# Retained values with tokens on the partitions: row sums as a column, division in ScalarE's copy, TensorE transposes back

## The reference, cut to what matters

```python
def _retention(x, wkqv):
    k, q, v = jnp.split(x @ wkqv, 3, axis=-1)
    qkt = jnp.einsum('bid,bjd->bij', q, k) / jnp.sqrt(jnp.float32(d))
    row_norm = 1.0 + jnp.sqrt(jnp.arange(s, dtype=x.dtype))[None, :, None]
    r = jnp.tril(qkt) / row_norm
    denom = jnp.clip(jnp.abs(r.sum(-1, keepdims=True)), 1.0, None)
    r = r / denom
    return jnp.einsum('bij,bjd->bid', r, v)

def block(h, p):
    r = _retention(h, wk)
    m = r @ w1 + b1
    a, gate = jnp.split(m, 2, axis=-1)
    m = a * jax.nn.silu(gate) @ w2 + b2
    m = _groupnorm1(m, gg, gb)
    y = m + h
    f = jax.nn.gelu(y @ wf1 + bf1_, approximate=False) @ wf2 + bf2_
    return (_layernorm(f + y, lg, lb), None)
```

## Time and profile before

| | before |
|---|---|
| median of three runs | 2643.9 us |
| profiled execution, time / span | 2644.7 / 2642.9 us |
| mean granted clock of TensorE | 0.978 |
| TensorE matmul / weight load busy | 94% / 78% |
| VectorE / ScalarE / GpSimd busy | 66% / 50% / 52% |
| retention layers | from 0 to about 1210 us |
| a regular body | 68.9 us |

### The profile page before, as it was taken

One profiled execution on the slowest core, in us unless ns is written; L12 is line 12 of the kernel. 1 busy time (PEld: TensorE's weight loads), 2 busy tenths in 40 slices (PEclk: granted clock), 3 DMA queues, 4 the chain that ended last, 5 costly groups with the idle time before them and its releaser, 6 DMA issues. The chain is left out here.

```text
span 2642.9 us, 35142 instructions
## 1 busy us (share of the span) xinstructions
PE 2493.1 (94%) x11574; PEld 2052.7 (78%) x11574; DVE 1739.8 (66%) x2906; ACT 1333.7 (50%) x2288; POOL 1362.8 (52%) x1258
## 2 busy tenths in 40 slices
PE   7999999999999999984899999999999999999997
PEld 5788778887888778862677778878888788888886
DVE  2677777778777877764667774656646556455445
ACT  3465655565555655543455554444444444444443
POOL 2244554444444554445577785455654546554544
PEclk9999999999999999996999999999999999999999
DMA  5100001001200010004565554443344434344441
GB/s 160 61 32 32 32 24 63 19 31 32 72 32 32 32 40 32 24 16 140 187 211 181 171 202 179 168 156 143 146 179 159 165 122 166 140 169 164 144 165 68
DMA packets 99962, 283.54 MB, mean 107 GB/s; under 512 B 6384, under 2 KB 76416, under 8 KB 83456
## 3 DMA queue, kind: packets, MB, share of 16 engines
q1 hardware_dynamic: 99712, 282.01, 30.7%
q10 hardware_dynamic: 128, 0.03, 0.0%
HBM read 212.42 MB, written 69.60 MB: 107 GB/s over the span
## 5 line engine op out<-in xcount | busy, mean ns | idle before, releaser
L1333 POOL TENSOR_TENSOR hid_lo<-full,hid_hi 128x512 fp32r<-128x512 f32 x384 | 498.4, 1311 | 569.4 <-ACT full L1436 459.4
L1614 DVE SCALAR_TENSOR_TENSOR full<-m_ps,bias_cols,sum 128x512 f32<-128x512 f32 x384 | 288.2, 750 | 215.5 <-PE m_ps L1715 201.5
L1713 PE MATMUL m_ps<-hid_hi,m_w 128*128 128x512 f32 x1024 | 403.5, 394 | 0.2 <-POOL hid_lo L1333 0.2
L1715 PE MATMUL m_ps<-hid_hi,m_w 128*128 128x512 f32 x1024 | 401.4, 392 | 0.0
L1714 PE MATMUL m_ps<-hid_lo,m_w 128*128 128x512 f32 x1024 | 401.3, 392 | 0.0
L1713 PE MATMUL m_ps<-m_t_hi,m_w 128*128 128x512 f32 x896 | 355.5, 397 | 27.8 <-DVE full L1614 17.5
L1714 PE MATMUL m_ps<-m_t_lo,m_w 128*128 128x512 f32 x896 | 351.6, 392 | 0.0
L1715 PE MATMUL m_ps<-m_t_hi,m_w 128*128 128x512 f32 x896 | 351.6, 392 | 0.0
L1433 ACT ACTIVATE hid_hi<-m_ps,bias_cols 128x512 fp32r<-128x512 f32 x128 | 88.3, 690 | 495.3 <-PE m_ps L1715 495.3
L322 POOL TENSOR_TENSOR pf_lo<-tmp,pf_hi 128x512 fp32r<-128x512 f32 x128 | 161.6, 1296 | 168.0 <-ACT pf_hi L498 168.0
L1440 ACT ACTIVATE hid_hi<-full 128x512 fp32r<-128x512 f32 x256 | 161.9, 632 | 164.0 <-DVE full L1614 163.8
(11 more groups left out here) (195 smaller groups left out, 5664.1 us busy)
## 6 DMA issues: line engine op xcount, KB each, us to landing
m_w<-prepared SPq DMA_DIRECT2D x96, 1408.0 KB, 6.0
prepared<-m_w SPq DMA_DIRECT2D x32, 1408.0 KB, 5.8
h_store<-h_out SPq DMA_DIRECT2D x32, 512.0 KB, 3.2
m_raw<-in_L_ffn_W SPq DMA_DIRECT2D x64, 256.0 KB, 6.4
gate_bc<-gate_rows SPq DMA_DIRECT2D x32, 512.0 KB, 6.7
h_in<-h_store SPq DMA_DIRECT2D x24, 512.0 KB, 4.3
h_in<-in_L_attn_x SPq DMA_DIRECT2D x8, 512.0 KB, 5.1
raw<-in_L_attn_Wf SPq DMA_DIRECT2D x8, 512.0 KB, 8.1
```

Source lines behind the costliest of these rows:

```text
L1333: nc.gpsimd.tensor_tensor(out=hid_lo[:, k, :], in0=full[:, k, :], in1=f32(hid_hi[:, k, :]), op=ALU.subtract).then_inc(hid_ready, 1)
L1614: nc.vector.scalar_tensor_tensor(out=full[:, k, :], in0=src, scalar=b1_col(e, 2 * fp + BLOCK_ROW[k]), in1=other[:, :], op0=ALU.add, op1=AL ...
L1713: nc.tensor.matmul(out, w[0], x[0], start=first, stop=False, skip_group_check=True)
L1715: return nc.tensor.matmul(out, w[1], x[0], start=False, stop=last, skip_group_check=True)
```

## The change

Retained values are now computed with tokens on the partitions. For each query block k, the stationary operand is the masked score block and the moving one is h, widened by a column of ones (and one for evenness), so that column 256 of the result is the row sum. VectorE makes divisor and reciprocal for 128 x 1 (or 128 x 2) values. ScalarE copies each block out of PSUM and scales it by the reciprocal of its token (`keep_r`). TensorE transposes the copies back (`transpose_r`), eight 128 x 128 blocks per slot. The products of `gated_projection` come out already divided, so `scaled` is gone, and silu and the gated product read PSUM. `up_projection` of slot B and the two calls of `down_projection` of slot A are parted, with `transpose_r` between their halves.

```diff
-        h_sp = split_tiles("h", [P, TB, D])
+        h_sp = split_tiles("h", [P, TB, D + 2])
+            def keep_r(s, at, blocks):
+                for k in blocks:
+                    act.wait_ge(scale_done[s], at.it * SCALE_CHAIN + (3 if k < 2 else 3 * k))
+                    nc.scalar.activation(r_tok[s][:, k, :], score_bank(s, k)[:, 0:D], ACT.Copy, scale=den[s][:, 1, k:k + 1]).then_inc(r_kept[s], 1)
             def high_r(s, at):
                 for c in range(DC):
-                    act.wait_ge(r_psum[s], at.base + 2 * c + 2)
+                    act.wait_ge(rT_psum[s], at.base + 2 * c + 2)
...
-                act.wait_ge(gate_scaled[s], at.base + 2 * c + 2)
-                nc.scalar.activation(tmp[s][:, 2 + c, :], tmp[s][:, 2 + c, :], ACT.Silu,
+                act.wait_ge(m_psum[s], at.base + 2 * c + 1)
+                nc.scalar.activation(tmp[s][:, 2 + c, :], bank(s, GATE[c]), ACT.Silu,
...
                     for c in range(DC):
                         high_y(B_, before, c)
+                    keep_r(A_, now, range(TB))
                     high_r(A_, now)
...
                 high_f(A_, now, FC - 1)
+                keep_r(B_, now, range(TB))
                 load_table(ACT.Silu)
                 high_r(B_, now)
...
-            def divisor(s, at):
...
+            def divide(s, at):
                 base = at.it * SCALE_CHAIN
...
+                for n, (k, width) in enumerate(((0, 2), (2, 1), (3, 1))):
+                    r = (2 + k) % 4
+                    sums = ps[:, 4 * s + r:4 * s + r + width, D]
+                    dve.wait_ge(r_psum[s], at.base + k + width)
+                    landed(nc.vector.tensor_tensor(out=den[s][:, 0, k:k + width], in0=sums, in1=floor[:, k:k + width], op=ALU.max),
+                           scale_done[s], base + 3 * n + 1)
+                    landed(nc.vector.scalar_tensor_tensor(out=den[s][:, 0, k:k + width], in0=sums, scalar=-1.0, in1=den[s][:, 0, k:k + width],
+                                                          op0=ALU.mult, op1=ALU.max), scale_done[s], base + 3 * n + 2)
+                    nc.vector.reciprocal(den[s][:, 1, k:k + width], den[s][:, 0, k:k + width]).then_inc(scale_done[s], 1)
...
             def gated_products(s, at, meanwhile=lambda part: None):
-                scaled(s, at, 0, GATE, 2, 1, gate_scaled)
-                scaled(s, at, 0, VALUE, 0, 2, value_scaled)
+                gated(s, at, 0)
                 meanwhile(0)
-                gated(s, at, 0)
-                scaled(s, at, 1, GATE, 2, 1, gate_scaled)
                 low_u(s, at, 0)
-                scaled(s, at, 1, VALUE, 0, 2, value_scaled)
                 gated(s, at, 1)
...
-                divisor(A_, now)
+                divide(A_, now)
                 low_r(A_, now)
-                invert(A_, now)
...
             def retain(s, at):
...
+                pe.wait_ge(h_lo[s], at.base + U)
+                for k in range(TB):
+                    pe.wait_ge(p_masked[s], at.base + k + 1)
+                    for b in range(k + 1):
+                        ins = mm3(score_bank(s, k)[:, 0:D + 2], both(pf_sp[s], ALL, b, cols(k)), both(h_sp[s], ALL, b), b == 0, b == k)
+                    ins.then_inc(r_psum[s], 1)
+
+            def transpose_r(s, at):
+                for k in range(TB):
+                    pe.wait_ge(r_kept[s], at.base + max(k + 1, DC))
                     for c in range(DC):
...
+                        ins = nc.tensor.transpose(bank(s, 2 + c)[:, cols(k)], r_tok[s][:, k, cols(c)], ident[:, :])
+                        if k == TB - 1:
+                            ins.then_inc(rT_psum[s], 2)
...
                 retain(A_, now)
                 if before:
-                    up_projection(B_, before)
+                    up_projection(B_, before, (0,))
                 else:
                     fold(2)
+                transpose_r(A_, now)
+                if before:
+                    up_projection(B_, before, (1,))
                 gated_projection(A_, now)
...
                 retain(B_, now)
-                for c in range(DC):
-                    down_projection(A_, now, c)
+                down_projection(A_, now, 0)
+                transpose_r(B_, now)
+                down_projection(A_, now, 1)
```

More of the change, by code:

```diff
@@ L124, in retention_layers @@
         z = slot_tiles("z", [P, TB, D])
-        inv = [t[:, 0, :] for t in y]
+        r_tok = [t[:, :, :].rearrange("p c (k d) -> p (c k) d", d=D) for t in y]
+        den = slot_tiles("den", [P, 2, TB])
         warm = sb("warm", [P, 1])
@@ L315, in _ @@
                                     base=0, pattern=[[-1, P]], channel_multiplier=1).then_inc(pool_consts, 1)
-            nc.gpsimd.memset(f32(ones_r[:, :]), 1.0).then_inc(pool_consts, 1)
+            for s in range(SLOTS):
+                nc.gpsimd.memset(f32(h_sp[s][0][:, :, D:D + 2]), 1.0).then_inc(pool_consts, 1)
+                nc.gpsimd.memset(f32(h_sp[s][1][:, :, D:D + 2]), 0.0).then_inc(pool_consts, 1)
             nc.gpsimd.memset(neg_half[:, :], -0.5).then_inc(pool_consts, 1)
             nc.gpsimd.memset(mean_w[:, :], 1.0 / (P * DC)).then_inc(pool_consts, 1)
-            pool.wait_ge(pool_consts, 5)
+            pool.wait_ge(pool_consts, 8)
             def low_half(lo, full, hi, done, n):
@@ L554, in body @@
                 else:
+                    keep_r(A_, now, range(TB))
+                    empty_fold(2)
                     high_r(A_, now)
-                    empty_fold(2)
                 load_table(ACT.Silu)
@@ L675, in gated @@
             def gated(s, at, c):
-                dve.wait_ge(value_scaled[s], at.base + 2 * c + 2)
+                dve.wait_ge(m_psum[s], at.base + 2 * c + 2)
                 dve.wait_ge(gate_ready[s], at.base + 2 * c + 2)
                 nc.vector.scalar_tensor_tensor(
-                    out=tmp[s][:, c, :], in0=tmp[s][:, c, :], scalar=lc_bm1[s][:, c:c + 1],
+                    out=tmp[s][:, c, :], in0=bank(s, VALUE[c]), scalar=lc_bm1[s][:, c:c + 1],
                     in1=tmp[s][:, 2 + c, :], op0=ALU.add, op1=ALU.mult).then_inc(u_ready[s], 2)
@@ L829, in body @@
                     layernorm_var(B_, before)
-                divisor(B_, now)
+                divide(B_, now)
                 low_r(B_, now)
-                invert(B_, now)
             def first(now):
@@ L929, in retain @@
             def retain(s, at):
-                def weighted_h(b):
-                    q = slice(LO[b], S)
-                    for c in range(DC):
[L934 to L945, removed]
-                    for half in range(2):
-                        ins = nc.tensor.matmul(bank(s, 0)[:, q], ones_r[:, :], pf_sp[s][half][:, b, q],
-                                               start=b == 0 and half == 0, stop=b == TB - 1 and half == 1,
-                                               skip_group_check=True)
-                ins.then_inc(rowsum_psum[s], U)
-                weighted_h(2)
-                weighted_h(3)
+                pe.wait_ge(h_lo[s], at.base + U)
[7 more added lines that the diff above has]
+                    pe.wait_ge(r_kept[s], at.base + max(k + 1, DC))
+                    for c in range(DC):
+                        ins = nc.tensor.transpose(bank(s, 2 + c)[:, cols(k)], r_tok[s][:, k, cols(c)], ident[:, :])
+                        if k == TB - 1:
+                            ins.then_inc(rT_psum[s], 2)
             def gated_projection(s, at):
@@ L977, in group_moments, with up_projection @@
                                  stop=True).then_inc(gn_psum[s], U)
-            def up_projection(s, at):
+            def up_projection(s, at, chunks=range(DC)):
                 w = weight("f1", DC)
                 pe.wait_ge(w_lo, split_count("f1", at.layer))
-                for k in range(DC):
+                for k in chunks:
                     pe.wait_ge(y_lo[s], at.base + 2 * k + 2)
```

33 lines of the change are left out of this document (9 added, 24 removed).

## The result

The changed kernel takes 2606.1 us (median of four runs, 2604.4 to 2607.3) against 2644.1 us (the kernel before, with one more run than above). The direction was right; several sizes were wrong.

A forecast was written before the change was run, and what follows sets the result against it. TensorE was taken to bound the retention layers. Twelve bodies at -1.35 - 0.68 + 1.2 give -10.0, seams +0.2, first step -0.7, tail -2.0: -12.5 us, so 2631 us against the median; range 2614 to 2652.

The forecast's parts named there:

- The wait in front of slot B's out projection, -1.35: Without the scalings VectorE's last low half arrives in time, margin 0.4 us, so TensorE's wait goes: -1.35 us per regular body.
- Rival B: The out projection still waits some 0.7 us per body as VectorE's low half lands late: 2642 us, no change; chance 0.20.
- Retain in slot B, -0.68: 30 matmuls of 258 columns take 3.57 us instead of 5.04, eight transposes add 0.79: net -0.68 us, no new wait.
- Slot A, +1.2: TensorE waits for VectorE's nine narrow steps and ScalarE's copy before the last transposes: slot A 1.2 us longer.
- a narrow step that the next waits for takes 0.27 us from start to start: VectorE's divisor steps in slot A: with the reciprocal at 0.16 us, 0.70 us per round, three rounds.
- rival A: The narrow steps are cheap: slot A costs 0.3 us instead of 1.2, time 2617 us; chance 0.17.
- over the 0.23: TensorE's undisturbed 512-column matmul was taken as 0.23 us from start to start; waits were counted beyond that.
- Seams, +0.1 each: In the three seams slot A is 2.1 us longer; with -1.35 and -0.68 that is +0.1 us each.
- in the seams I count the same 1.35: The removed out projection wait of slot B was counted in seams at the regular body's 1.35 us.
- First step -0.7, tail -2.0: The first step's slot B saves 0.7 us, its slot A 0; in the tail two scalings and blocking go, -2.0.
- Rival C, the clock: TensorE's clock falls in slot A after the new wait, costing at least 2.8 us; slower, 2673 us; chance 0.15.
- If that were enough in every body: Condition for the clock's fall: a wait of 1.2 to 1.5 us at eight transposes suffices in every body, giving 2673 us.

The follow-up runs named there:

- e3: The kernel before without its four scalings per slot, gate and product reading PSUM, the division left out: 2613.2 us (ratio 0.9887).
- after, gap 384: The changed kernel with 384 unused bytes per partition between the weights and the slots' tiles: 2621.8 us (ratio 0.9928).
- e8: The changed kernel with each of the three narrow rounds of the division done twice, 18 narrow steps per slot instead of nine: 2639.5 us (0.9986).
- e4: The changed kernel with VectorE's nine narrow steps of slot A moved ahead of the last low half of slot B's group norm: 2596.4 us (0.9821).
- e12: The changed kernel with 256 instead of 258 columns in retain, so the row sums are left out: 2604.1 us.
- e2: The kernel before with an unused tile of 32 bytes per partition that moves its large tiles to multiples of 64 bytes: 2641.8 us (0.9996).
- e7: The changed kernel with three more wide VectorE steps per slot (maximum, scaled maximum, reciprocal) behind the low half of r: 2694.4 us (1.0192).

## Why the prediction was wrong

The first body's start and the clock in seams differ by 1 to 3 us between profiles of like kernels, so the terms outside the regular bodies are known to that.

- *The wait in front of slot B's out projection, -1.35:* right. It measured -1.43 in the changed kernel (4.28 to 2.85 us for its 12 matmuls) and -1.50 in e3. Rival B is wrong: no wait is left. The last low half lands at 451.89, 1.0 us before TensorE wants it at 452.93, where the walk of the chain left 0.4.
- *Retain in slot B, -0.68:* right. With the old pace (after, gap 384) the stretch from B to A is 0.60 shorter. No wait took its place.
- *Slot A, +1.2:* mis-sized, about +0.65 at the old pace. The step that failed is "a narrow step that the next waits for takes 0.27 us from start to start", with the reciprocal at 0.16: in this chain the first is 0.19, and behind a reciprocal that the next step does not wait for only 0.09. The nine steps took 1.44 us instead of 2.1. The copies, taken as 0.45 us each, ran at 0.39 (1.57 for four), and only the last one counted. So the truth lies some six tenths of the way to rival A. The mechanism stood: e8 shows the chain on the path, e4 takes it off. Over 12 bodies this is 7 us of the miss.
- *The pace of the 512-column matmuls, no term at all:* this is the main step that failed. It is -0.8 us per body. After with 384 bytes takes 2621.8 us, with none 2606.1: 16 us of the 25 that were missed, the largest part. The prediction took the earlier trace rows's "over the 0.23" as a constant of the chip. The widening of h by two columns was counted as columns of retain, not as bytes that move every tile behind it.
- *Seams, +0.1 each:* wrong, they gave 2.9, 3.6 and 3.7 us. Of that the pace is some 0.9. The step that failed is "in the seams I count the same 1.35": e3 shows 3.1 us there without the clock, as VectorE is late in a seam at more places than this one. The prediction has no term for the clock in seams either: it fell behind the wait of 2.6 us in all three seams of the kernel before, but in the changed kernel only in the first. Seams without a fall compare as 74.8 and 72.7 us, 2.1 less. No run shows that the change keeps the clock up there: in e12, with the same wait of 2.6 us, the same two seams had a fall and took 75.5 and 74.3 us.
- *First step -0.7, tail -2.0:* -3.9 and -2.2. The first step takes 82.3 to 84.8 us over the profiles of the kernel before and its shifted forms, and 79.4 to 81.0 over those of the changed one; partly this is the pace. The tail differs by 1.4 to 3.0 us over the same profiles, which fits its forecast but does not test it.
- *Rival C, the clock:* did not come in regular bodies. The waits around the transposes were 0.8 us; e8 shows it at 2.3. "If that were enough in every body" was too strong: it came in three bodies of twelve.

Between the two profiles the retention layers gave 42.7 us, 30 more than the sum: 16.4 in the twelve regular bodies (9.8 by the pace, 6.6 by slot A), 10.4 in the seams and 3 in the first step. The scatter of the rest of the span took 5 of them back, and 25 remain.

With the old pace, a regular body gives 1.44 us instead of 0.83, and the whole kernel 2621.8: inside the range, 9 us from the forecast. What put it outside was one mechanism that none of the rivals held. That the pace helped, and did not hurt, is luck of the layout; by the terms that were forecast the direction holds without it.

## What to carry to other kernels

Where the tensor engine is the bound, compare the pace of untouched matmuls before and after, not only waits: a change of a tile's size moves all tiles behind it, and 2% of pace in 190 matmuls was worth 0.8 us of a body here, over half of the 1.4 us that the removed wait gave. Try a few gaps of 32 to 256 bytes between the stationary and the moving tiles before judging any other change. When a producer's chain lands just late, look for idle time of its engine ahead of the last unrelated step, as between sum and low half here.

## What the runs showed of the hardware

- TensorE, 512 columns fp32r, 128x128 weights: 0.2278 us from start to start at distances of 0 modulo 256 bytes between weight and moving tile, 0.2332 at 32, 0.2290 at 64 and 0.2324 at 128 (means over the retention layers; 0.2268 in a steady stretch at 0). The absolute address did not matter (shifts of 32, 2,528 and 2,560 bytes of both).
- VectorE: dependent narrow steps 0.19 us apart, one that does not wait for the step before it 0.09. Wide 128x512 steps with two operands in SBUF took up to 2.79 us beside GpSimd instead of 0.69, and ended about 0.6 us behind the end of GpSimd's step (464.62 + 1.99 in the earlier trace rows, 2.75 and 2.79 in e7).
- The granted clock stood at 0.57 over a 4 us window after transposes with waits of 2.3 us around them (e8), in three of twelve like bodies, and stayed whole in all twelve with 0.8 us (after). Behind a wait of 2.57 us without transposes it fell to 0.50 (before, first seam) or stayed at 1.00 (e2, the same seam of the same program).
